# A decoder on one core: in the cross attention, the eight PSUM banks are shared out anew (four in the ring for exponentials and turnings, three for scores, one for values), the score maxima are taken bank by bank, and the query and key stacks are turned at other steps

## The reference

```python
def _L0_xattn_ref(q, k, v):
    B, S, E = (2, 512, 512)
    QH, KVH = (32, 8)
    D = E // QH                  # 16
    G = QH // KVH                # 4
    b, s, _ = q.shape            # 4, 512
    qh = q.reshape(b, s, KVH, G, D).transpose(0, 2, 3, 1, 4)
    kh = k.reshape(b, s, KVH, D).transpose(0, 2, 1, 3)
    vh = v.reshape(b, s, KVH, D).transpose(0, 2, 1, 3)
    scale = 1.0 / jnp.sqrt(jnp.float32(D))
    scores = jnp.einsum('bkgsd,bktd->bkgst', qh, kh) * scale
    attn = jax.nn.softmax(scores, axis=-1)
    out = jnp.einsum('bkgst,bktd->bkgsd', attn, vh)
    return out.transpose(0, 3, 1, 2, 4).reshape(b, s, E)
...
x = x + _L0_xattn_ref(_layernorm(x, axis=-1), ctx_512, ctx_512)
```

## Time and profile before

| | us |
|---|---|
| median of 3 runs | 3188.11 (3188.07 to 3188.22) |
| the profiled execution's own time | 3187.65 |
| its span in the trace | 3186.3 |
| first score matmul of the cross attention | 587.5 |
| last `settle` turning of the cross attention | 1041.0 |
| TensorE busy over the span | 2942.8 (92%) |
| VectorE busy over the span | 2046.5 (64%) |
| ScalarE busy over the span | 1637.4 (51%) |

### The profile page before, as it was taken

How to read it: one execution, slowest core, us unless ns; L and a number is a source line. 1 busy time by engine, 2 the same in 40 slices (tenths; PEclk the granted TensorE clock), 3 DMA queues, 4 the chain that set the end, 5 groups by cost and what they waited for, 6 DMA issues and landing times.

```text
span 3186.3 us, 47057 instructions
## 1 busy us (share of the span) xinstructions
PE 2942.8 (92%) x17001; PEld 1976.8 (62%) x17001; DVE 2046.5 (64%) x3519; ACT 1637.4 (51%) x2990; POOL 1110.4 (35%) x1150
## 2 busy tenths in 40 slices
PE   7898987899999779999997999999999999988897
PEld 3344433333333448888865888888888888855565
DVE  3454455678876768777766455565555666548786
ACT  1223222377777437777742443444455455447775
POOL 2343333334321023333335444454544344322210
PEclk8999999799999889999997999999999999989999
DMA  3000000000000138875663012121123143020000
GB/s 127 1 1 1 1 1 1 8 6 6 2 2 2 69 125 317 333 254 192 212 207 97 21 50 71 54 67 54 54 90 116 50 130 109 25 86 11 11 14 21
DMA packets 125913, 238.86 MB, mean 75 GB/s; under 512 B 14282, under 2 KB 73247, under 8 KB 119284
## 3 DMA queue, kind: packets, MB, share of 16 engines
q1 hardware_dynamic: 102020, 119.95, 11.6%
q0 software_dynamic: 22512, 113.80, 10.4%
q10 hardware_dynamic: 1152, 2.10, 0.2%
HBM read 223.99 MB, written 40.63 MB: 83 GB/s over the span
## 4 chain that ended last, share of the span: by engine, by line
PE 58%; DVE 13%; ACT 8%; issue 5%; DMA 1%; POOL 1%; SPq 0%; POOLq 0%; ACTq 0%; DVEq 0%; another core or an unknown queue 0%
PE ps L1634 9%; PE ps L1636 9%; PE ps L1635 9%; PE ps L879 4%; PE ps L890 4%; PE ps L2897 3%; DVE d_PTl L2483 2%; DVE d_mx L2468 2%; PE ps L2872 2%; PE ps L2907 2%; ACT d_PTh L2335 1%; PE ps L1648 1%; DVE d_qk L2460 1%; ACT d_qk L2320 1%; PE ps L843 1%
## 5 line engine op out<-in xcount | busy, mean ns | idle before, releaser
L2669 POOL TENSOR_SCALAR d_P<-d_P,d_rv 128x128 f32<-128x128 f32 (+3 forms) x256 | 289.8, 1144 | 582.8 <-DVE d_rv L2476 582.5
L1009 DVE TENSOR_REDUCE b_mx<-ps 128x2 f32<-128x1024 f32 x256 | 307.8, 1220 | 82.0 <-PE ps L868 81.4
L953 ACT ACTIVATE b_PT<-ps 128x512 f32<-128x512 f32 x512 | 273.5, 600 | 22.6 <-PE ps L879 21.4
L2328 ACT ACTIVATE d_P<-ps,d_nb 128x128 f32<-128x128 f32 (+3 forms) x256 | 135.1, 528 | 245.6 <-DVE d_nb L2470 241.4
L879 PE MATMUL ps<-b_Q,b_KT 64*128 64x512 f32 x512 | 205.5, 467 | 15.5 <-ACT b_PT L953 15.2
L1634 PE MATMUL ps<-d_xh,d_wh 128*128 128x512 f32 x512 | 215.2, 420 | 1.4 <-DVE d_xl L2445 1.4
L2483 DVE TENSOR_TENSOR d_PTl<-ps,d_PTh 128x384 fp32r<-128x384 f32 (+1 forms) x192 | 114.6, 597 | 157.3 <-ACT d_PTh L2335 157.3
L868 PE MATMUL ps<-b_KT,b_Q 64*128 64x512 f32 x512 | 205.1, 484 | 6.4 <-DVE b_mx L1009 5.8
L1635 PE MATMUL ps<-d_xl,d_wh 128*128 128x512 f32 x512 | 204.2, 399 | 0.0
L1636 PE MATMUL ps<-d_xh,d_wl 128*128 128x512 f32 x512 | 203.7, 398 | 0.0
L1815 DVE TENSOR_TENSOR x_wl<-x_wr,x_wh 128x1024 fp32r<-128x1024 f32 x126 | 149.6, 1222 | 45.3 <-ACT x_wh L1723 45.3
(11 more groups left out here) (487 smaller groups left out, 8502.9 us busy)
## 6 DMA issues: line engine op xcount, KB each, us to landing
eoscr<-x_eo SPq DMA_DIRECT2D x87, 256.0 KB, 4.6
d_w<-in_L_attn_W_Q SPq DMA_DIRECT2D x32, 256.0 KB, 3.8
d_w<-in_L_attn_W_K SPq DMA_DIRECT2D x32, 256.0 KB, 4.6
d_w<-in_L_attn_W_V SPq DMA_DIRECT2D x32, 256.0 KB, 5.3
d_wo<-in_L_attn_W_O SPq DMA_DIRECT2D x16, 512.0 KB, 4.8
d_cmb<-in_wgT SPq DMA_DIRECT2D x16, 512.0 KB, 4.9
d_cmb<-in_wuT SPq DMA_DIRECT2D x16, 512.0 KB, 4.6
d_cmb<-in_wdT SPq DMA_DIRECT2D x16, 512.0 KB, 3.9
```

Source lines behind the costliest of these rows:

```text
L953: e.activation(M.PT[:, half, v % 2, 2 * p + y, :], ps[:, O.bank(("ex", v, y)), :], ACT.Exp, scale=0.25).then_inc(S["b_ex"], 1)
L1009: e.tensor_reduce(M.mx[:, r % 2, q, :], ps[:, 2 * (t % 2):2 * (t % 2) + 2, :], AX.X, ALU.max).then_inc(S["b_mx"], 1)
L2669: e.tensor_scalar(P, P, M.rv[:, y, q:q + 1], None, ALU.mult).then_inc(S["d_nm"], 1)
```

## The change

`SCORES` is now banks 0, 1 and 2 and `RING` is banks 3, 4, 5 and 6, so `room` waits for the use four places back. Scores take their three banks in turn, one score after the other: score c = 2t + 1 - h waits for the maxima of score c - 3. VectorE takes the maxima of each bank by an instruction of its own, as soon as that score is there; GpSimd's `parts` waits for eight of them instead of four. The query stacks are turned at steps 1 and 5 of an item instead of 2 and 6, the key stacks at steps 0 and 7 instead of 1 and 5. The number of matmuls stays as it was, VectorE gets 512 reductions of 128x512 for 256 of 128x1024.

```diff
--- before.py
+++ after.py
@@ -707,7 +707,8 @@
 
     LAG = 14
     DEEP = 6
-    RING = (4, 5, 6)
+    SCORES = (0, 1, 2)
+    RING = (3, 4, 5, 6)
 
     def __init__(self):
         self.work = [(b, g) for b in range(B) for g in range(8)]
@@ -722,7 +723,7 @@
                     self.order += [("ex", v, 0), ("ex", v, 1)]
         self.index = {u: k for k, u in enumerate(self.order)}
 
-    FIRST = [("keys", 0, t, h) for t in range(4) for h in range(2)][0:5]
+    FIRST = [("keys", 0, t, h) for t in range(4) for h in range(2)][0:4]
 
     def step(self, n, s):
         if n < 0:
@@ -730,11 +731,11 @@
         out = []
         if n < self.N:
             b, g = self.work[n]
-            if b + 1 < B and 2 <= g <= 5 and s in (1, 5):
-                out.append(("keys", b + 1, g - 2, s // 4))
-            if s == 2:
+            if b + 1 < B and 2 <= g <= 5 and s in (0, 7):
+                out.append(("keys", b + 1, g - 2, s // 7))
+            if s == 1:
                 out.append(("one", 2 * n + 1))
-            if s == 6 and n + 1 < self.N:
+            if s == 5 and n + 1 < self.N:
                 out.append(("one", 2 * n + 2))
             if s == 7:
                 out.append(("top", 2 * n))
@@ -746,8 +747,13 @@
 
     def bank(self, use):
         if use in self.FIRST:
-            return (0, 1, 2, 3, 7)[self.FIRST.index(use)]
-        return self.RING[self.index[use] % 3]
+            return (*self.SCORES, 7)[self.FIRST.index(use)]
+        return self.RING[self.index[use] % len(self.RING)]
+
+    @staticmethod
+    def score(t, h):
+
+        return 2 * t + 1 - h
 
     def release(self, use):
 
@@ -821,8 +827,8 @@
 
     def room(use):
         m = O.index[use]
-        if m >= 3:
-            sem, n = O.release(O.order[m - 3])
+        if m >= len(O.RING):
+            sem, n = O.release(O.order[m - len(O.RING)])
             e.wait_ge(S[sem], n)
         return ps[:, O.bank(use), :]
 
@@ -856,16 +862,15 @@
     def scores(t, h):
         n, s = t // 8, t % 8
         b, g = O.work[n]
-        r, q = 2 * n + s // 4, s % 4
-        if h == 1:
-            if q == 0:
-                e.wait_ge(S["b_one"], r + 1)
-                if g == 0:
-                    e.wait_ge(S["b_key" if b else "b_key0"], 8 * max(b, 1))
-            if t >= 2:
-                e.wait_ge(S["b_mx"], t - 1)
+        r, q, c = 2 * n + s // 4, s % 4, O.score(t, h)
+        if h == 1 and q == 0:
+            e.wait_ge(S["b_one"], r + 1)
+            if g == 0:
+                e.wait_ge(S["b_key" if b else "b_key0"], 8 * max(b, 1))
+        if c >= 3:
+            e.wait_ge(S["b_mx"], c - 2)
         rows = slice(64 * h, 64 * h + 64)
-        e.matmul(ps[:, 2 * (t % 2) + h, :], M.Q[rows, r % O.DEEP, q * 128:q * 128 + 128], M.KT[rows, b % 2, g, :], start=True, stop=True).then_inc(S[f"b_sc{h}"], 1)
+        e.matmul(ps[:, O.SCORES[c % 3], :], M.Q[rows, r % O.DEEP, q * 128:q * 128 + 128], M.KT[rows, b % 2, g, :], start=True, stop=True).then_inc(S[f"b_sc{h}"], 1)
 
     def exps(v, y):
         j, s = v // 8, v % 8
@@ -1002,11 +1007,11 @@
             if n < O.N:
                 t = 8 * n + s
                 r, q = t // 4, t % 4
-                e.wait_ge(S["b_sc1"], t + 1)
-                e.wait_ge(S["b_sc0"], t + 1)
                 if q == 0 and r >= 2:
                     e.wait_ge(S["b_parts"], r - 1)
-                e.tensor_reduce(M.mx[:, r % 2, q, :], ps[:, 2 * (t % 2):2 * (t % 2) + 2, :], AX.X, ALU.max).then_inc(S["b_mx"], 1)
+                for h in (1, 0):
+                    e.wait_ge(S[f"b_sc{h}"], t + 1)
+                    e.tensor_reduce(M.mx[:, r % 2, q, h:h + 1], ps[:, O.SCORES[O.score(t, h) % 3], :], AX.X, ALU.max).then_inc(S["b_mx"], 1)
 
 
 def cross_pool(e, S, M, G):
@@ -1043,7 +1048,7 @@
     def parts(r):
         cols = M.nr[:, r % 2, 0:16].rearrange("p (h a q) -> p a h q", h=2, a=2)
         src = M.mx[:, r % 2, :, :].rearrange("p q h -> p h q")
-        e.wait_ge(S["b_mx"], 4 * r + 4)
+        e.wait_ge(S["b_mx"], 8 * r + 8)
         if r >= 2:
             e.wait_ge(S["b_topp"], r - 1)
         t = po.inc(e.tensor_scalar(cols[:, 0, :, :].bitcast(FR), src, -1.0, None, ALU.mult))
```

## The result

| | before | after |
|---|---|---|
| median, same chip, 4 runs each | 3188.09 (3185.58 to 3188.22) | 3159.25 (3147.88 to 3161.04) |
| ratio of the times | | 0.9907, interval 0.9892 to 0.9922 |
| the profiled execution's own time | 3187.65 | 3159.59 |
| span | 3186.3 | 3158.3 |
| first score to last settling | 453.5 | 425.5 |

The change made the kernel 28.8 us faster. All of the difference between the profiled executions (28.06) lies in the stage (28.0). That the two agree so closely is luck: the time outside the stage is 2732.8 us in both, but ranges from 2725 to 2743 over the profiles of all kernels here. A row "from one item's first values to the next's" is the lap as the prediction uses it; I read it from the first of each item's four groups of values.

What follows compares the result with a forecast made beforehand. TensorE was taken to bound the stage, waiting 1.41 us per 13.19 us lap for the ring. Terms 18.4 (plain laps), 4.6 (key laps), 0 (ten laps) and -0.9 (start) sum to 22.1 gained: median 3166, range 3161 to 3180.

Steps and rivals of the forecast that it cites:

- laps without keys or statistics: Fifteen laps of the stage, each to fall from 13.19 to 11.96 us, a gain of 1.23 each, 18.4 together.
- laps with keys and no statistics: Five clean laps with key turnings, each to fall from 14.04 to 13.12 us, 0.92 each, 4.6 together.
- laps with statistics: Six items where VectorE sets the pace: 0.53 us more each, 3.2 in all, offset by four key laps behind them.
- start: First 14 steps, scores alone: 28 reductions at 0.60 take 16.8 us for 15.9, a loss of 0.9.
- 1.41 us of ring waits: TensorE's waits in a 13.19 us lap for the ring of three; with a ring of four all should go.
- ScalarE's order: Rival "nothing comes of it": ScalarE's order, not the ring, holds the pairs; lap stays 13.19, total 3188; chance 0.07.
- the chain that the prediction built: Score waits for maxima of c - 3: bank free after 1.22 us, but two bare steps would give only 0.91.
- pair to values: 0.43 (705.80 to 706.23): TensorE's distance from a pair's start to the values', one of the unit prices summed to an 11.78 us lap.
- the chain of the score banks at step 7: Across the top at step 7: score bank free after 1.22 us, needed after 1.25, so it suffices by 0.03.
- Ten laps at zero: Six items with statistics lose 3.2 us, the four clean key laps behind them get 3.6 back; counted as zero.
- The dearer-reduction rival: A one-bank reduction keeps VectorE up to 0.71 us instead of 0.60; 4.3 us gained, total 3184; chance 0.19.
- the slower one: Rival: VectorE becomes the bound; at 0.75 us per reduction the kernel is 13.7 us slower, 3202; chance 0.06.

Runs made afterwards that it cites:

- the 16-column run: Changed kernel plus a write of 128x16 zeros to an unused tile on VectorE behind each of the 512 reductions; 3160.51 us, ratio 0.9913.
- the four spread: Changed kernel with the next batch's four statistics taken one at a time at steps 0, 2, 4, 6 instead of in a row; 3148.6 us, ratio 0.9885.
- the run at 0.852: Changed kernel plus a write of 128x288 zeros behind each reduction, reductions 0.852 us from start to start; 3241.86 us, ratio 1.0191.

## Why the prediction was off

The sum on record against the traces, us gained:

| term | forecast | measured |
|---|---|---|
| laps without keys or statistics (14, and the last two intervals) | 18.4 | 14 x 1.47 + 1.8 = 22.4 |
| laps with keys and no statistics (ten) | 4.6 | 14.4 |
| laps with statistics (five, and one in the start) | 0 | -5.1 |
| start | -0.9 | -4.2 |
| behind the last values | | +0.5 |
| sum | 22.1 | 28.0 |

The forecast's 4.6 is five laps with keys at 0.92. It counted four more, behind those with statistics, as zero, and left one out: there are ten (g = 2 to 5 of the first batch, g = 2, 3 and 5 of the next two).

**The mechanism was right.** All 1.41 us of ring waits went; a ring of three in the changed kernel brings the old stage back to within 0.3 us, though the clean lap stays 0.45 shorter than before, so the ring of four, added last, is 1.02 of the lap's 1.47. ScalarE's order was not what held the pairs. The moved turnings are needed with three score banks (13.1 us), by the chain that the prediction built.

**The step that failed first: "pair to values: 0.43 (705.80 to 706.23)".** I took that distance for a property of the two instructions and carried it into the new lap. The pair at 705.80 was itself late. Those rows had a second value, too: 0.49 (701.99 to 702.48), behind a pair that was later still. Of the 117 groups of values that start between 620 and 990 us in the new trace, 86 start 0.31 to 0.33 behind a pair that itself comes 0.34 after the one before. 19 start 0.42 or 0.43 behind the score of a split pair. Ten start 0.40 or 0.41 behind a pair that is on time and not split; all ten stand at step 7 of a lap with keys. In the run with a ring of three the same instructions are 0.42 to 0.44 apart behind late pairs, and 0.32 or 0.33 behind eleven of the few on time. So ending the waits gave 0.11 more per group than the waits themselves, about 8 us over the stage by my estimate (14 plain laps x 0.33, ten with keys x 0.36). Three groups of a plain lap: 11.96 - 3 x 0.11 = 11.63; the late score of step 7 adds 0.05; measured 11.72. With keys, three groups give 0.33 and the fourth 0.03, and the keys' turning ahead of a top takes 0.49 + 0.21 where I had 0.58 + 0.25, which is 0.13: 13.12 - 0.49 = 12.63; measured 12.67. The rows of such a step 7, with one of the ten at 0.41:

```profile
650.09 0.66 PE L842 MATMUL ps<-cst,b_KS 128*128 128x128 f32 x4
650.58 0.27 PE L854 MATMUL ps<-cst,b_nr 128*128 128x128 f32 x1
650.79 0.50 PE L884 MATMUL ps<-b_Q,b_KT 64*128 64x512 f32 x1
...
651.12 0.47 PE L884 MATMUL ps<-b_Q,b_KT 64*128 64x512 f32 x1
...
651.53 1.07 PE L895 MATMUL ps<-b_PT,b_V 128*32 128x512 f32 x8
```

What in the machine makes the 0.11, and why the ten differ, is not shown by any run.

**A small term: the chain of the score banks at step 7.** I wrote 1.22 against 1.25. It is 0.56 + 0.68 + 0.07 = 1.31 against 1.26: I left out the time from a reduction's end to the score that it lets go. So the score is 0.05 late where I had 0.03 to spare.

**"Ten laps at zero" was wrong in both directions.** The four laps with keys behind the statistics gained 1.39 each like the others, 5.6 together. Of those with g = 4 two stayed (14.25 to 14.35) and the one without keys gained 0.5 (13.63 to 13.14), where I had a loss of 0.53 in each. The laps with the row of statistics lost 2.0 and 3.3: I counted elements on VectorE and left out that TensorE runs ahead of it by three scores where it could by four. VectorE is away for three us, a score waits 2.2 with all of TensorE's work behind it, and in most cases the clock falls. These laps have 4.7 and 6.0 over a plain one. By the lap of the 16-column run without a fall (14.89) 3.2 of it is the wait with what goes with it, 1.5 is 3.4 us at 1.2 GHz, and 2.8 is 6.8 us. With the four spread, both the long wait and the low clock are gone. The prediction priced the chain of score banks in plain laps alone.

**The start cost 4.2, not 0.9.** I priced reductions back to back, but they aren't: they wait 0.86 after two turnings of queries (0.48 and 0.50 before), and the row of statistics makes a score wait 1.84 (1.51 before), at the 1.2 GHz level. With the statistics spread the start is 28.28, with the old steps 28.66, with four score banks and a ring of three 27.53, of which 3.4 us ran at the full clock. The changed kernel itself has 29.58 and 30.15 in its two profiles, so 0.6 is the least that can be told apart. The rest of the loss, more than two us over the old 25.34, is in every kernel with single reductions and is not parted further.

**Right, with their numbers:** a reduction of 0.68 and 0.60 apart; VectorE is no bound of plain laps (three more levels of price show where it would be); no pair of a clean lap waits for an exponential (0.2 us of idle time in all 512 of them); waits as instructions cost nothing seen. The dearer-reduction rival and the slower one failed on the price: the run at 0.852 shows that the slower one's mechanism is real.

The misses partly cancel. Plain laps gave 4.0 more than forecast and laps with keys 9.8 (5.6 of it in the four counted as zero, about 1.4 in the one left out), the laps with statistics and the start 5.1 + 3.3 less, the end 0.5 more: 5.9. So the four laps counted as zero and the laps with statistics nearly cancel by luck, and what is left over is mostly the price of values behind a pair.

## What to carry to other kernels

A distance between two instructions that is read behind a late one holds the lateness; read unit prices only where everything ahead was on time, or the gain of removing waits comes out too small. When buffers are moved from one queue to another, look at the giving side for the longest stretch in which its reader does something else, not at the usual lap. Here cutting such a block on a shared engine into single instructions gave 8.7 us of stage with three score banks, 2.4 with four.

## What the runs showed of the chip

- The same group of values (matmuls into 32-column strips) starts 0.31 to 0.33 us after a pair of 64-row matmuls that came on time in 86 cases and 0.40 or 0.41 in ten; it starts 0.42 to 0.49 after one that was late or split.
- Small writes on VectorE behind a one-bank reduction add less than their rows last: 16 columns add 0.01, 96 add 0.05, 288 add 0.25 to the distance of the reductions (0.60), while their rows say 0.07, 0.14 and 0.30.
- An idle time of TensorE of 2.2 to 2.4 us in an otherwise dense stretch came with 3.4 or 6.8 us at 1.2 GHz in seven cases of eight (two each in the changed kernel, its repetition, and the runs with 16 and 96 columns). Shorter ones did so too, if less often: 1.3 us once of two (four score banks), 1.5 once of two (ring of three), 1.6 in neither of two (old steps). Alone, idle times of 0.4 to 0.6 did not. Two close together did (0.49 and 0.62, in the laps with g = 4 of the run with 288 columns): 3.4 us, both times.
